# A tower of embedding, recurrence and mixture-of-experts on one core: a start written out as its own program, one copy on ScalarE moved behind another, and an end that stays on VectorE

## The reference

```
h  = patches(x) @ tok_W.T + tok_b                     # [16, 784, 64], K = 64
xn = layernorm(h)
s_t = tanh(xn_t @ W_ih.T + b_ih + s_{t-1} @ W_hh.T + b_hh)     # t = 0..15
h  = h + s
x2 = layernorm(h)
logits = x2 @ gate_w + gate_b                         # 16 experts, the best 2, softmax over them
moe = sum over the 2 best of w * (relu(x2 @ w1[e] + b1[e]) @ w2[e] + b2[e])
out = h + (layernorm(x2 + moe) * gamma + beta)
```

## Time and profile before

| | |
|---|---|
| median of 3 runs (lowest to highest) | 567.13 us (566.46 to 568.65) |
| the profiled execution | 566.65 us, its span 564.8 us |
| busy: PE, PEld, DVE, ACT, POOL | 510.9, 335.2, 418.1, 353.2, 158.5 us |
| mean granted TensorE clock | 0.981 |
| chain that ended last, by engine | PE 77%, DVE 9%, ACT 7%, issue 4%, POOL 2% |

### The profile page before, as it was taken

How to read it: one execution, slowest core, us unless ns; L and a number is a source line. 1 busy time by engine, 2 the same in 40 slices (tenths; PEclk the granted TensorE clock), 3 DMA queues, 4 the chain that set the end, 5 groups by cost and what they waited for, 6 DMA issues and landing times.

```text
span 564.8 us, 8784 instructions
## 1 busy us (share of the span) xinstructions
PE 510.9 (90%) x3030; PEld 335.2 (59%) x3030; DVE 418.1 (74%) x835; ACT 353.2 (63%) x612; POOL 158.5 (28%) x130
## 2 busy tenths in 40 slices
PE   3467999999999999999999999999999999999972
PEld 2345666566666666566665666666575656656641
DVE  1243988796969789696969789696978879796771
ACT  3235575675858575675858666676758567666552
POOL 4112021422313141332324141331314142231234
PEclk9997999999999999999999999999999999999995
DMA  7109266754819184664819284573909275565601
GB/s 166 32 4 203 77 143 141 159 125 117 176 56 229 36 195 99 140 139 100 199 36 221 60 179 118 123 157 79 217 25 216 64 150 120 132 147 117 148 1 46
DMA packets 29627, 69.04 MB, mean 122 GB/s; under 512 B 6416, under 2 KB 8336, under 8 KB 29456
## 3 DMA queue, kind: packets, MB, share of 16 engines
q1 hardware_dynamic: 29584, 68.49, 53.0%
HBM read 60.39 MB, written 8.08 MB: 121 GB/s over the span
## 4 chain that ended last, share of the span: by engine, by line
PE 77%; DVE 9%; ACT 7%; issue 4%; POOL 2%; POOLq 0%; DVEq 0%; ACTq 0%
PE pZ L726 29%; PE pO L739 28%; PE pA L752 5%; ACT hexp L430 4%; PE pA L653 3%; PE pA L683 3%; DVE acc L569 2%; DVE prod L553 2%; PE pB L653 2%; POOL inv_std L327 2%; PE pA L671 2%; PE pB L710 2%; PE pA L698 1%; PE pA L663 1%; ACT h L374 1%
## 5 line engine op out<-in xcount | busy, mean ns | idle before, releaser
L430 ACT ACTIVATE hexp<-pZ,b1c 128x784 f32<-128x784 f32 x256 | 225.5, 910 | 110.4 <-PE pZ L726 110.4
L726 PE MATMUL pZ<-xt,w1hi 128*128 128x392 f32 x512 | 192.0, 375 | 13.5 <-ACT hexp L430 13.4
L739 PE MATMUL pO<-hexp,w2s 128*64 128x392 f32 x1024 | 199.6, 506 | 0.9 <-DVE prod L553 0.5
L553 DVE SCALAR_TENSOR_TENSOR prod<-pO,b2c,spread 128x392 f32<-128x392 f32 x256 | 149.7, 621 | 51.9 <-PE pO L739 51.8
L726 PE MATMUL pZ<-xt,w1lo 128*128 128x392 f32 x512 | 175.1, 342 | 0.0
L327 POOL TENSOR_TENSOR inv_std<-var,nhalf 112x7 f32<-112x7 f32 x48 | 75.2, 1568 | 245.2 <-DVE var L487 245.2
L726 PEld LDWEIGHTS pZ<-xt,w1hi 128*128 128x128 f32 x512 | 97.2, 190 | 62.9 <-issue 34.8
L569 DVE TENSOR_TENSOR acc<-acc,prod 128x784 f32<-128x784 f32 x112 | 122.1, 1090 | 0.1
L739 PEld LDWEIGHTS pO<-hexp,w2s 128*64 128x64 f32 x1024 | 70.5, 136 | 77.1 <-issue 62.4
L726 PEld LDWEIGHTS pZ<-xt,w1lo 128*128 128x128 f32 x512 | 97.6, 191 | 0.0
L487 DVE TENSOR_REDUCE var<-sq 112x7 f32<-112x455 f32 x48 | 29.9, 624 | 59.0 <-ACT sq L386 48.8
(11 more groups left out here) (78 smaller groups left out, 455.1 us busy)
## 6 DMA issues: line engine op xcount, KB each, us to landing
spread<-gates_dram SPq DMA_DIRECT2D x128, 392.0 KB, 9.0
h_dram<-h SPq DMA_DIRECT2D x16, 248.1 KB, 2.4
h2c<-h_dram SPq DMA_DIRECT2D x16, 248.1 KB, 6.2
xcur<-x_in SPq DMA_DIRECT2D x16, 196.0 KB, 6.2
out<-yo SPq DMA_DIRECT2D x16, 196.0 KB, 5.5
w1f<-w SPq DMA_DIRECT2D x2, 512.0 KB, 6.1
w2s<-w SPq DMA_DIRECT2D x1, 512.0 KB, 4.3
gates_dram<-gt SPq DMA_DIRECT2D x16, 28.0 KB, 2.0
```

What stands on the lines that cost most here:

```text
L430: nc.scalar.activation(hexp[u % RING][:, :].rearrange("p (b c) -> p b c", b=2), halves(pZ[u % 2]), ACT.Relu, bias=b1c[:, u:u + 1]).then_in ...
L553: nc.vector.scalar_tensor_tensor(out=prod[q % RING][:, b * HALF:(b + 1) * HALF], in0=halves(pO)[:, b, :], scalar=b2c[:, q:q + 1], in1=spre ...
L726: last = nc.tensor.matmul(halves(pZ[e % 2])[:, b, :], w[:, e, :], xt[par][:, b * HALF:(b + 1) * HALF], start=(k == 0), stop=(k == 1))
L739: last = nc.tensor.matmul(halves(pO)[k * D:(k + 1) * D, b, :], w2s[:, e, :], hexp[e % RING][:, b * HALF:(b + 1) * HALF], start=True, stop= ...
```

## The change

- **The fill.** The bodies t = -2 and t = -1 are gone, and each engine has a list of its own for steps 0, 1 and the embedding of 2, ahead of body(0). Steps 1 and 2 are embedded into pZ[0] (`wide_z`), and xn of step 1 is turned in pZ[1]; these are the banks of the first layer, which is not yet running. The split of w1 into high and low part is made in two halves. The gating of step 0 stands on DVE directly behind its x2, and the square of h2 of step 0 on ACT no longer behind the copies of the next embedding. In body(0) DVE, ACT and PE treat step 1 later: x2 at u = 2, its low part at u = 3 behind the first product, gating at u = 4 and 6, `x2_turn(1)` at u = 5.
- **The chains of semaphores** are cut finer: EMBED ends with rstd, TURN and STATE take over, with the waits that this needs.
- **In each body** the high part of x2 (ACT) goes from u = 14 to u = 15, behind the relu of expert 15; `gates_turn` and the copy of gt from u = 10 to u = 11.
- **The end.** The last add before the last product is put ahead of it; `last_sum_turn` sums the last product on PE (first the seven tiles of acc, then the seven of prod onto them) where DVE had added it. The scale, gamma and beta are six DVE instructions where they had been seven on ACT and four on POOL, and the output is stored in two parts of 4 and 3 tiles. h2 of the last step is fetched earlier.

```diff
+        def embedded_in(s):
+            return wide_z if s in (1, 2) else wide
+
+        def xn1_turned_in(s):
+            return pZ[1] if s == 1 else pA
...
         def run(eng, body):
-            body(-2, 0, mix=True, embed=True)
-            body(-1, 1, gate=True, mix=True, embed=True)
             body(0, 0, experts=True, gate=True, mix=True, embed=True)
...
         @block.sync
...
+            load_x(2)
+            load_x(3)
+            for dst, src in expert_loads:
+                sp.dma_start(dst, src).then_inc(experts_loaded, 16)
+            keep_h2(0)
+            spread_gates(0, 0)
+            keep_h2(1)
             run(sp, body)
-            fetch_h2(STEPS - 1)
-            store(STEPS - 1)
-            sp.wait_ge(stored, 16 * STEPS + 16)
+            for stage, some in zip(("out_a", "out_b"), LAST_PARTS):
+                LAST.wait(sp, 0, stage)
+                sp.dma_start(out[STEPS - 1, :, some, :], yo[:, some, :]).then_inc(stored, 16)
+            sp.wait_ge(stored, 16 * STEPS + 32)
...
         @block.scalar
...
-                    if gate and u == at(t, 10, first=12, fill=5):
...
+                    if gate and u == at(t, 11, first=13):
+                        keep_gt(t + 1)
...
+                    if known(t, 1) and u == 2:
+                        high_part(t + 1)
+                    if mix and u == 15:
+                        high_part(t + 2)
                     if close and u == 15:
                         close_norm(t - 1)
-                    if mix and u == 14:
-                        MIX.wait(act, t + 2, "x2")
-                        nc.scalar.activation(x2hl[:, :, 0, :], x2[:, :, :], ACT.Copy).then_inc(MIX.sem, 1)
...
+            keep_h1(1, 1)
+            square_h1(1, 1)
+            w1_high_part(0)
+            keep_xn1t(0)
+            w1_high_part(1)
             act.wait_ge(rb_set, 1)
+            new_hidden(0)
+            keep_xn1t(1)
+            square_h2(0)
+            new_hidden(1)
+            high_part(0)
+            keep_h1(2, 0)
+            square_h1(2, 0)
+            keep_xt(0, 0)
+            exp_gap(0)
+            keep_gt(0)
+            relu(0, 0)
+            relu(0, 1)
+            square_h2(1)
             run(act, body)
...
         @block.vector
...
+            scale_h1(0, 0)
+            norm_var(EMBED, 1, 0)
+            scale_h1(1, 1)
+            w1_low_part(0)
+            w1_low_part(1)
+            add_state(0, 0)
+            norm_var(MIX, 0, 1)
+            norm_scale(MIX, 0, 1, x2[:, :, :], h2[:, :, 0:D])
             dve.wait_ge(rank_set, 1)
+            bias_logits(0)
+            find_first(0)
+            low_part(0)
+            find_second(0)
+            norm_var(EMBED, 2, 0)
+            gate_weights(0)
+            add_state(1, 1)
+            norm_var(MIX, 1, 1)
+            scale_h1(2, 0)
             run(dve, body)
             last = STEPS - 1
+            add(last, Q - 2, last % 2)
             product(last, Q - 1, last % 2)
-            add(last, Q - 2, last % 2)
-            add(last, Q - 1, last % 2)
-            norm_var(CLOSE, last, 2)
...
+            norm_var(LAST, 0, 2)
+            nc.vector.tensor_tensor(yn[:, :, :], cen[:, :, :], over_tiles(gam[:, :], D), ALU.mult).then_inc(gamma_applied, 1)
...
+            norm_scale(LAST, 0, 2, yn[:, :, :], yn[:, :, :])
...
+            for some in LAST_PARTS:
+                nc.vector.tensor_tensor(yo[:, some, :], yn[:, some, :], h2b[:, some, :], ALU.add).then_inc(LAST.sem, 1)
...
         @block.tensor
...
+            def last_sum_turn(s, par):
...
+                pe.wait_ge(summed, n)
...
+                for i in range(TILES):
+                    nc.tensor.matmul(tiles_of(pA)[:, i, :], acc[par][:, i * P:(i + 1) * P], fold[:, 0:D],
+                                     start=(i == 0), stop=False)
+                pe.wait_ge(p_ready, 2 * n + 2)
+                for i in range(TILES):
+                    last = nc.tensor.matmul(tiles_of(pA)[:, i, :], prod[(Q - 1) % RING][:, i * P:(i + 1) * P],
+                                            fold[:, 0:D], start=False, stop=(i == TILES - 1))
+                last.then_inc(LAST.sem, 1)
```

More of the change, by code:

```diff
@@ L144, in vit_tower_kernel, with at @@
         CLOSE = Chain("close_stage", "turned center square var rstd norm gamma out")
-        def at(t, steady, first=None, fill=None):
-            slot = fill if known(t, 0) else first if known(t, 1) else None
-            return steady if slot is None else slot
+        LAST = Chain("last_close_stage", "turned center square var rstd norm out_a out_b")
+        def at(t, steady, first=None):
+            return first if first is not None and known(t, 1) else steady
         embed_loaded = sem("embed_weights_loaded")
@@ L326, in rstd @@
                 chain.wait(pool, s, "var")
+                if chain is EMBED and not known(s, 1):
+                    TURN.wait(pool, s - 1, "norm")
                 nc.gpsimd.tensor_tensor(inv_std[:, lane, :], var[:, lane, :], nhalf[:, :], ALU.pow)\
@@ L371, in keep_h1 @@
                 if not known(s, 2):
-                    MIX.wait(act, s - 2, "h2")
-                for some, fresh in wide:
+                    STATE.wait(act, s - 2, "h2")
+                for some, fresh in zip(some_tiles, embedded_in(s)):
                     nc.scalar.activation(h1[par][:, some, :], fresh, ACT.Copy).then_inc(h1_kept, 1)
@@ L405, in keep_xn1t @@
             def keep_xn1t(s):
-                EMBED.wait(act, s, "turned")
+                turned = xn1_turned_in(s)
+                TURN.wait(act, s, "turned")
                 if not known(s, 1):
-                    MIX.wait(act, s - 1, "pre")
+                    STATE.wait(act, s - 1, "pre")
                 if known(s, 1):
                     act.wait_ge(consts, STATE_SET)
-                nc.scalar.activation(state[D:2 * D, 1, 0:REST], pA[D:2 * D, 0:REST], ACT.Copy).then_inc(EMBED.sem, 1)
@@ new lines, in keep_gt, with square_h2, w1_high_part @@
+            def keep_gt(s):
+                GATE.wait(act, s, "turned")
+                if not known(s, 1):
+                    act.wait_ge(gt_stored, 32 * s)
+                nc.scalar.activation(gt[:, :], pB[0:2 * E, 0:FIRST], ACT.Copy).then_inc(GATE.sem, 1)
+            def square_h2(s):
+                STATE.wait(act, s, "h2")
+                nc.scalar.activation(sq[:, 1, :, 0:D], h2[:, :, 0:D], ACT.Square, scale=D ** -0.5).then_inc(MIX.sem, 1)
+            def w1_high_part(k):
+                act.wait_ge(gate_loaded, GATE_LOADED)
+                some = w1_parts[k]
+                nc.scalar.activation(w1hi[:, some, :], w1f[:, some, :], ACT.Copy).then_inc(w1_high, 1)
@@ L609, in body @@
                         norm_var(CLOSE, c, 2)
-                    if embed and u == at(t, 13, fill=15):
+                    if embed and u == 13:
                         norm_var(EMBED, a, 0)
@@ L613, in body @@
                         norm_scale(MIX, s, 1, x2[:, :, :], h2[:, :, 0:D])
[L614 to L617 removed]
+                    if mix and u == 15:
+                        low_part(s)
             dve.wait_ge(consts, EPS_SET)
@@ L720, in first_layer @@
                 if known(n, 1):
-                    pe.wait_ge(w1_split, 2)
+                    pe.wait_ge(w1_low, 2)
+                    pe.wait_ge(h1_kept, 2 * 2 + 2)
+                if known(n, 2) and not known(n, 1):
+                    TURN.wait(pe, 1, "xn1t")
                 if not known(n, 2):
@@ L775, in body @@
                         hidden_turn(t + 2)
-                    if embed and u == at(t, 9, first=11, fill=7):
+                    if embed and u == at(t, 9, first=11):
                         embed_in(t + 3)
@@ L779, in body @@
                         sum_turn(t - 1, 1 - par, embed, mix)
-                    if gate and u == at(t, 1, first=3):
+                    if gate and not known(t, 1) and u == 1:
                         x2_turn(t + 1)
             embed_in(0)
+            embed_in(1)
             pe.wait_ge(consts, IDENT_SET)
+            embed_turn(0)
             pe.wait_ge(cell_loaded, CELL_LOADED)
+            recur(0)
+            embed_turn(1)
+            hidden_turn(0)
+            recur(1)
+            embed_in(2)
+            x2_turn(0)
+            first_layer(0, 0, 0)
+            gates_turn(0, True)
+            first_layer(0, 1, 0)
+            hidden_turn(1)
             run(pe, body)
             second_layer(STEPS - 1, Q - 1)
-            sum_turn(STEPS - 1, (STEPS - 1) % 2)
+            last_sum_turn(STEPS - 1, (STEPS - 1) % 2)
 def kernel(**inputs):
```

204 lines of the change are left out of this document (120 added, 84 removed).

## The result

| | before | after |
|---|---|---|
| median, us (lowest to highest of 4) | 566.80 (566.23 to 568.65) | 535.44 (534.79 to 535.65) |
| after / before (95% interval) | | 0.9439 (0.9416 to 0.9463) |
| profiled span, us | 564.8 | 533.9 |
| first part, to `x2_turn(2)` | 80.11 | 72.08 |
| middle, `x2_turn(2)` to `x2_turn(15)` | 415.43 | 397.03 |

The kernel is 31.4 us faster; 28.5 were forecast (the prediction's sum of 28.8 starts from the median of 567.1 that it had). The cuts of the lower rows are the starts of `x2_turn` on PE in the two traces (80.11 and 495.54 before, 72.08 and 469.11 after), so the three add up to the span: 8.0 came in the fill with body(0), 18.4 in the middle and 4.5 at the end, against 11.2, 12.2 and 5.4. The total is near the forecast by luck: a term that was too small and two that were too large nearly cancel.

The account below looks back on a forecast made before the run. PE was taken to bound the steady step (busy 31.02 of 32.09 us), with chains in fill and end. Savings of 11.2 (fill), 12.2 (middle) and 5.4 (end) sum to 28.8, giving 538.3 us; range 533.5 to 547.

Parts of the forecast that it names:

- The middle, 12.2 forecast: Steady steps: 11.6 us from moving the high part, 1.8 from later `gates_turn`, less 1.2 for DVE; 12.2 us saved.
- the charge of 1.2 for DVE: Steady steps: DVE's back-to-back chain before product 1 only partly keeps up with earlier PE; 0.1 us a step lost.
- POOL's gamma beside DVE's norm: Body's end: earlier gamma may slow DVE's norm by up to 1.0 us, a later add regains 0.8; counted as cancelling.
- The fill, 11.2 forecast: Fill and body(0): shorter chain brings expert 6's first layer from 57.46 to 46.3; 11.2 us saved.
- "I expect no worse": Fill: PE seldom idle over 1 us from 30.4 on, so its clock gets no worse; throughout at 1.2 GHz, about 2 more.
- The end, 5.4 forecast: Kernel's end: product and turn 2.8 us earlier, finish 2.75 instead of 4.2 us; sum 5.5, taken as 5.4 saved.
- "Now one add (0.96) goes first": Kernel's end: one 0.96 us add precedes the last product, which ends at 549.9 while PE turns acc beside it.
- The late spread: Rival, fill: first spread pair lands at 9.0 or PE stays at 1.2 GHz; fill gives 7, total 542.5 us; 15%.
- that the fill would not be shorter: Rival, fill: ACT's long written list holds the chain as before; total 549.5 us; 4%.
- the returned stall: Rival, steady steps: DVE has no room, second layers wait for products, only fill and end gain; 550.5 us; 10%.
- the half clock at the end: Rival, end: both halves of the last turn take twice as long, the end gives 2.5; total 541.2 us; 8%.
- The slower rival: Steady steps: high part ending over 1.5 us after first layer 0 costs one for one; up to 573.7 us; 3%.

Follow-up runs that it names:

- b_high: Kernel before with only the high part of x2 moved behind the relu of expert 15 in the bodies from 0 on: 551.49 us, ratio 0.9733.
- a_high14: Changed kernel with the high part of x2 put back at u = 14, nothing else: 551.36 us, ratio 0.9722.
- e_prod_first: Changed kernel with the last product ahead of the last add, and PE turning the product's tiles first, acc's second: 533.69 us, ratio 0.9392.
- a_high_late: Changed kernel with the high part of x2 one place later, behind `close_norm`: 535.32 us, ratio 0.9446.
- a_high_u0: Changed kernel with the high part of x2 behind relu 0 of the next body: 548.15 us, ratio 0.9646.
- f_low: Changed kernel with the low part of x2(1) ahead of the first product in body(0): 531.36 us, ratio 0.9366.
- f_turn: f_low_gate with step 0's gating exponential ahead of the xt copies and `gates_turn(0)` ahead of first layer 0 in the fill: 532.53 us, ratio 0.9372.
- best: f_low_gate with the end of e_prod_first: 530.46 us, ratio 0.9340.
- f_exp: Changed kernel with the exponential of step 0's gating ahead of the two copies of xt on ACT: 535.38 us, ratio 0.9435.
- a_oldend: Changed kernel with the old end put back, one store, and h2 of the last step fetched late again: 538.36 us, ratio 0.9489.
- f_low_gate: f_low with the logits' bias and first half of step 1's gating also ahead of the first product: 531.45 us, ratio 0.9368.

## Why the prediction was right in sum, and where its steps were wrong

**The middle, 12.2 forecast, 18.4 found: the mechanism right, the term mis-sized.** The prediction took 12 x 0.93 + 0.41 for the high part. The runs with the high part alone (b_high, a_high14) show 15.2 and 15.9, and 14.8 and 14.5 in the middle of their traces: a stall costs its idle time plus the overlap that PE's matmuls lose when they restart. From the start of first layer 0 to that of the next second layer it was 2.81 us before (271.24 - 268.43) and is 1.64 after (254.51 - 252.87): 1.17 less, which is the 1.15 of the period. `gates_turn`: 0.14 x 13 = 1.8 forecast, 4.0 measured, for the same reason and in a larger proportion. And the charge of 1.2 for DVE was not needed: no second layer waits for a product in the steady steps after (the group of L858 has 0.6 us of idle time in the whole run).

**POOL's gamma beside DVE's norm** was right as a balance, wrong as a mechanism. The prediction let the norm of xn take up to 1.0 more and the add give 0.8 back. The norm took 0.62 and the add became 0.96; gamma took 1.68 and the output add went from 1.15 to 2.05; and the 0.8 that DVE has to pay it pays at the bias of the logits (1.10, not 0.28). In the places read here the one that comes while the other works pays: before, DVE's add, 0.13 behind POOL's; after, POOL's, 0.11 behind DVE's, and then DVE's bias beside that same output add; in e_prod_first POOL's, 0.08 behind. How long the one that waits is held differs: gamma waited through three DVE operations that follow each other without a pause in a_high_late, the output add in after through one; after a pause of 0.20 it was DVE that paid in a_high_u0. The groups show it over the run: the adds' mean was 1090 ns and is 1003, the median of the bias was 275 ns and is 1097. The Trainium skill ("GPSIMD Engine Reference", Key points) says that the two share their SBUF interfaces and contend when DVE reads two SBUF inputs. The trace agrees, with these numbers; who pays is read from the rows.

**The fill, 11.2 forecast, 8.0 found** (7.3 to 9.8 with the two other traces of the same text). The chain was the one forecast, with product 0 ahead of the low part. Three sizes were off, all behind the issue of `spread`: the landing (43.1, not 42.3), and from start to next start `x2_turn` (1.50, not 0.7) and the second layer (2.81, not 1.5): in the timeline they start at 44.87 and 46.37, and expert 6 at 49.18. The two last are the clock: "I expect no worse" was the step that failed. PE's pause of 2.77 came from a wait that the prediction had itself named, while it counted on pauses of seldom more than 1. It put expert 6 at 46.3; it stands at 49.18, and f_low, which takes the pause away, has it at 46.22. That a shorter pause is always enough is not shown: f_turn fell to the half clock after 0.84.

**The end, 5.4 forecast, 4.5 by the traces (2.9 to 4.3 by the old end put back).** Start of the last second layer to centre took 8.02 before and 6.23 after: 1.8 gained, where 2.8 were forecast. "Now one add (0.96) goes first" failed: the add that goes first is the second of a pair, and it starts (521.40) while POOL's gamma works, so it takes 1.72 and the pair 2.78, as long as in the earlier trace rows. The last product ends 4.2 after the last second layer starts (524.17 - 520.00), where the forecast comes to 3.3. The finish was sized well: from the centre to the end of the span 10.2 before and 7.7 after (533.9 - 526.23), 2.5 gained with 2.6 forecast, though the power takes 1.79, not 1.49, beside DVE's gamma.

**The rivals.** The late spread was partly true (0.8 of its 3.4, with PE at 1.2 GHz as its other half); that the fill would not be shorter was refuted by its 8.0; the returned stall was refuted by the 1.4 us of idle time; the half clock at the end is not in after, but is in f_low (last half 2.66 in place of 1.54). The slower rival's mechanism exists, as a_high_u0 shows, at a point at least 0.25 later than I had it. At 2.55 it costs 1.06 a step, of which 0.20 is the lateness itself; most of the rest is contention of DVE and POOL.

## What to carry to other kernels

Price a stall of a pipelined PE by start-to-start distances with and without it, not by its idle time: here 0.93 idle was 1.15, 0.14 was 0.30, and 0.77 and 0.19 were 0.84 and 0.23. Where a chain waits for a DMA, look for what is queued behind the waiting instruction without needing it; moving one such line up gave 4.1 us here, while the pair itself landed no earlier. When DVE and POOL meet, let the one that has no slack start first; at the end that gave 0.7 in the trace. And before a difference between two traces is put down to an edit, look whether it begins ahead of the edit: the issue of `spread` moved by 1.2 us, and PE's change from half to full pace in the fill by 5 us, between traces whose text is the same up to there.

## What the runs showed of the hardware that I had not expected

- The store of gt ahead of `spread` took 2.93 in after and 3.14 in best, 1.76 in f_low, f_exp, a_oldend and e_prod_first. The landing of the first pair did not follow: issued at 36.80, 36.97, 35.69, 35.59, 35.62 and 35.70, product 0 could start at 43.12, 43.31, 43.98, 43.53, 42.88 and 44.16 in these traces. What holds either was not tried.
- The profile's granted clock reads 1.00 in the fill while PE runs at half pace. In after the first layers 0 and 1 (from 30.08 to 33.4) have starts 0.33 apart, as at 49 where the clock reads 0.50; from 34.94 on they are 0.18 apart. In f_low and f_exp, whose text on PE is the same, the half pace lasts to 38. There the starts tell the level, and the record does not.
- After a pause of 1.63 us ahead of the turn at the end, the second half of the turn took 1.54 in after, a_high_late and f_low_gate, and 2.66, 2.46 and 2.53 in f_low, f_exp and f_turn. The same text behind the same pause is at either level; the first half took 1.59 in all six. Behind 0.88, in e_prod_first and best, the second half took 1.54 both times.
- A power of 112x7 on POOL takes 1.48 to 1.49, and 1.79 where DVE's operation runs beside it.
